# Gate folded into the output and query projections of a cross-attention block with a mixture of experts

## The reference

```python
# _layernorm(x): (x - mean) / sqrt(var + 1e-5)
x = x + xattn(ctx, ctx, _layernorm(x), mask, wq, bq, wk, bk, wv, bv, wo, bo)   # 16 heads of 16, ... @ wo_w + wo_b
x = x + ffn(_layernorm(x), rms_w, gate_w, W1, b1, W2, b2)

# inside ffn
xn = x * rsqrt(mean(x * x) + 1e-6) * rms_w
logits = xn @ gate_w.T                       # 8 experts
scores = softmax(logits)
top1_idx, top1_score = argmax(scores), max(scores)
ye = silu(xn @ W1[e] + b1[e]) @ W2[e] + b2[e]     # e = top1_idx, F = 1024
out = ye * top1_score
```

## Time and profile before

| | |
|---|---|
| median of 3 runs | 920.2 us (919.24 to 921.61) |
| the profiled execution | 914.09 us, its span 912.3 us |
| PE busy | 802.1 us, 88% |
| DVE busy | 620.0 us, 68% |
| POOL busy | 444.6 us, 49% |
| ACT busy | 430.2 us, 47% |
| chain that ended last, by engine | PE 33%, SP's queue 16%, POOL 16%, DMA 15%, issue 10%, DVE 7% |

### The profile page before, as it was taken

How to read it: one execution, slowest core, us unless ns; L and a number is a source line. 1 busy time by engine, 2 the same in 40 slices (tenths; PEclk the granted TensorE clock), 3 DMA queues, 4 the chain that set the end, 5 groups by cost and what they waited for, 6 DMA issues and landing times.

```text
span 912.3 us, 28391 instructions
## 1 busy us (share of the span) xinstructions
PE 802.1 (88%) x8764; PEld 586.7 (64%) x8764; DVE 620.0 (68%) x1898; ACT 430.2 (47%) x1004; POOL 444.6 (49%) x566
## 2 busy tenths in 40 slices
PE   1678999999999999999999999998627999999994
PEld 0445666666666666666666666665415888888783
DVE  4567777777777777777777877776374666665542
ACT  0235555555555555555555565554403333333331
POOL 0255644565445564456544665465416555556311
PEclk9989999999999999999999999999857999999998
DMA  4465676656776567765777567764153222223200
GB/s 134 108 169 134 171 175 182 177 142 169 180 186 175 142 164 181 204 195 153 196 191 215 165 168 193 195 189 120 32 195 95 77 82 82 81 79 97 71 29 7
DMA packets 107139, 130.01 MB, mean 143 GB/s; under 512 B 12942, under 2 KB 93704, under 8 KB 106569
## 3 DMA queue, kind: packets, MB, share of 16 engines
q1 hardware_dynamic: 100936, 116.38, 47.4%
q0 software_dynamic: 5600, 12.87, 4.7%
q10 hardware_dynamic: 544, 0.00, 0.0%
HBM read 94.07 MB, written 36.06 MB: 143 GB/s over the span
## 4 chain that ended last, share of the span: by engine, by line
PE 33%; SPq 16%; POOL 16%; DMA 15%; issue 10%; DVE 7%; ACT 1%; POOLq 1%; DVEq 0%
DMA arena_w<-in_x 14%; PE ps L1218 12%; PE ps L1236 10%; POOL arena_w L595 6%; SPq L476 5%; SPq L471 5%; POOL arena_b L583 3%; POOL arena_w L602 2%; POOL arena_w L584 2%; POOL arena_b L559 2%; SPq L440 1%; DVE arena_b L1351 1%; PE ps L1018 1%; POOL arena_b L584 1%; PE ps L994 1%
## 5 line engine op out<-in xcount | busy, mean ns | idle before, releaser
L744 ACT ACTIVATE arena_b<-ps 128x448 f32<-128x448 f32 (+1 forms) x384 | 194.0, 540 | 120.0 <-PE ps L980 119.1
L1369 DVE CUSTOM_DVE_ANT_0 arena_w<-ps,arena_w 112x375 bf16<-112x375 f32 x256 | 140.5, 549 | 47.4 <-PE ps L954 41.3
L976 PE MATMUL ps<-arena_b,arena_w 128*128 128x448 bf16 x384 | 136.6, 356 | 7.7 <-DVE arena_b L1378 5.6
L557 POOL TENSOR_TENSOR arena_b<-arena_b,arena_w 112x1 f32<-112x1 f32 x32 | 6.1, 190 | 279.8 <-DVE arena_b L1353 279.8
L1369 DVE CUSTOM_DVE_ANT_0 arena_b<-ps,arena_w 112x375 bf16<-112x375 f32 x256 | 139.8, 546 | 0.1
L980 PE MATMUL ps<-arena_b 128*128 128x224 f16 x768 | 136.2, 259 | 0.0
L1218 PE MATMUL ps<-arena_b,w_parts 128*128 128x256 f16 (+1 forms) x1056 | 109.2, 254 | 0.5 <-issue 0.3
L1218 PEld LDWEIGHTS ps<-arena_b,w_parts 128*128 x1056 | 90.8, 98 | 17.4 <-issue 2.9
L980 PEld LDWEIGHTS ps<-arena_b 128*128 128x128 f16 x768 | 75.2, 98 | 39.4
L994 PE MATMUL ps<-arena_b 128*17 128x112 f32 (+1 forms) x3072 | 99.4, 261 | 0.1
L1236 PE MATMUL ps<-arena_w,arena_b 128*128 x840 | 95.2, 273 | 0.1
(11 more groups left out here) (187 smaller groups left out, 1344.1 us busy)
## 6 DMA issues: line engine op xcount, KB each, us to landing
arena_b<-k_spill SPq DMA_DIRECT2D x128, 192.0 KB, 3.8
arena_b<-in_L_ffn_W SPq DMA_DIRECT2D x64, 256.0 KB, 4.5
arena_b<-q_spill SPq DMA_DIRECT2D x128, 112.0 KB, 4.2
k_spill<-arena_b SPq DMA_DIRECT2D x32, 384.0 KB, 5.0
arena_b<-in_ctx SPq DMA_DIRECT2D x32, 256.0 KB
arena_w<-in_x SPq DMA_DIRECT2D x64, 112.0 KB, 4.6
q_spill<-arena_w SPq DMA_DIRECT2D x32, 224.0 KB, 2.1
rows<-arena_w SPq DMA_DIRECT2D x32, 224.0 KB, 2.3
```

Of the source, the lines that this page charges most:

```text
L744: nc.scalar.activation(probsT[u % PROB_BUFFERS][0:n], scoreT_bank[c][0:n, 0:QUAD * T], ACT.Exp, scale=1.0 / SCALE_SCORES).then_inc(probs_r ...
L976: pe.matmul(bank[:, 0:QUAD * T], mask_keys[:, quad, c, :], max_rows[par].rearrange("p h t -> p (h t)"), start=True, stop=False)
L1369: nc.vector.tensor_tensor_reduce(out=masked_scores[r % 2], in0=shared_bank[r][0:T, 0:S], in1=mask_bias, scale=-1.0, scalar=3.4e38, op0=ALU ...
```

## The change

The logits are linear in x1, so they need not be computed from the normalised rows. With G the gate times rms_w, and G' the same with the mean over the 256 rows taken off each column, x1 @ G' equals (x1 - mean(x1)) @ G. The second scale is one factor per token, which changes no order among the 8 logits; it is needed only in the softmax value. x1 is x + attention @ wo + bo + (values' bias part). So:

- In setup G' is computed (a matmul with a constant 1/256, a subtraction), then wo @ G', which is appended to wo as 8 more columns, and a bias row; this needs wo transposed and one more load of bo.
- `project_attention` yields 264 columns; the last 8 are the attention's part of the logits.
- `project_queries` multiplies the transposed normalised x by G' too (8 columns). Normalised x is (x - mean) / std, so the result is multiplied by std, which POOL makes as variance times 1/std. DVE's `gate_of_x` does this and adds the bias row; `add_residual` adds the attention's part.
- The transposes, the gate's matmuls and two ACT copies per batch are gone; ACT keeps the factor of each batch (`copy_factor`), and POOL multiplies all logits by it once, before the exponential.

```diff
-        wo_sb = carve("a", P, DT, D)
+        wo_sb = carve("a", P, DT, WO_COLS)
# SP, setup
+            sp.dma_start(bo_cols, bo.rearrange("(t p) -> p t", p=P),
+                         allow_slow_non_contiguous=True).then_inc(weights_loaded, 16)
# POOL
-            def queries_rstd(b):
+            def queries_rstd(b, par):
...
                 pool.tensor_tensor(rstd, var1, minus_half, ALU.pow).then_inc(rstd_ready, 1)
+
+                wait_count(pool, gate_x_ready, b - 1)
+                pool.wait_ge(rstd_ready, b + 1)
+                pool.tensor_tensor(std1[par], var1, rstd, ALU.mult).then_inc(std_ready, 1)
...
+            pool.wait_ge(ln2_copied, B)
+            pool.wait_ge(logits_centred, 1)
+            pool.tensor_tensor(gate_exp, gate_exp, ln2_all[:, :].unsqueeze(2).to_broadcast([T, B, EXPERTS]),
+                               ALU.mult).then_inc(logits_centred, 1)
# ACT, setup and steps
+            nc.scalar.activation(woT.rearrange("p t n -> p (t n)"), scoreT_bank[0][:, 0:DT * D], ACT.Copy
+                                 ).then_inc(woT_copied, 1)
...
+            nc.scalar.activation(gate_bias, scoreT_bank[1][0:T, 0:EXPERTS], ACT.Copy).then_inc(setup_copied, 1)
...
-            def copy_routed(st):
...
-            def copy_gate(st):
...
+            def copy_factor(st):
                 b = st.batch(3)
+                wait_apart(act, ln2_rstd, b + 1, act_passed)
+                nc.scalar.activation(ln2_all[:, bass.ds(b, 1)], ln2, ACT.Copy).then_inc(ln2_copied, 1)
# PE, setup
+            for t in range(DT):
+                mm = pe.matmul(scoreT_bank[1][:, 0:EXPERTS], average, gw_sb[:, t], start=t == 0, stop=t == DT - 1)
+            mm.then_inc(gate_mean_ready, 1)
...
+            pe.wait_ge(wo_gate_copied, 1)
+            for j in range(DT):
+                pe.matmul(scoreT_bank[1][0:T, 0:EXPERTS], bv_rep[:, j, :], wo_sb[:, j, D:], start=j == 0, stop=False)
+            for j in range(DT):
+                mm = pe.matmul(scoreT_bank[1][0:T, 0:EXPERTS], bo_rep[:, j, :], gate_centre[:, j], start=False,
+                               stop=j == DT - 1)
+            mm.then_inc(gate_bias_ready, 1)
             pe.wait_ge(setup_copied, N_SETUP_COPIED)
# PE, scores of quad 3
                         pe.wait_ge(q_low_ready, DT * (b + 2))
+                        pe.wait_ge(gate_x_ready, b + 2)
                     if st.exists(2):
                         pe.wait_ge(x1_ready, st.batch(2) + 1)
-                    if st.exists(3):
-                        pe.wait_ge(xrT_copied, st.batch(3) + 1)
+                        pe.wait_ge(gate_added, st.batch(2) + 1)
# PE, project_queries
+                for k in range(DT):
+                    mm = pe.matmul(proj_bank[0][0:T, DT * T:DT * T + EXPERTS], xnT[:, k, :], gate_centre[:, k],
+                                   start=k == 0, stop=k == DT - 1)
                 mm.then_inc(queries_ready, 1)
# PE, project_attention
-                    mm = pe.matmul(tail_bank[0:T, 0:D], attT[:, j, :], wo_sb[:, j, :],
+                    mm = pe.matmul(tail_bank[0:T, 0:WO_COLS], attT[:, j, :], wo_sb[:, j, :],
...
-            def transpose_routed(st):
...
-            def gate(st):
# DVE, setup
+            nc.vector.tensor_copy(bo_rep, bo_cols.unsqueeze(2).to_broadcast([P, DT, T])).then_inc(const_dve, 1)
...
+            dve.wait_ge(gate_mean_ready, 1)
+            nc.vector.tensor_tensor(gate_centre, gw_sb, scoreT_bank[1][:, 0:EXPERTS].unsqueeze(1).to_broadcast(
+                [P, DT, EXPERTS]), ALU.subtract).then_inc(gate_centred, 1)
# DVE, steps
+            def gate_of_x(st):
+
+                b, par = st.batch(-1), st.parity(-1)
+                dve.wait_ge(std_ready, b + 1)
+                wait_apart(dve, queries_ready, b + 1, dve_passed)
+                nc.vector.scalar_tensor_tensor(
+                    out=gate_logits[:, bass.ds(b, 1), :].rearrange("p o e -> p (o e)"),
+                    in0=proj_bank[0][0:T, DT * T:DT * T + EXPERTS], scalar=std1[par], in1=gate_bias,
+                    op0=ALU.mult, op1=ALU.add).then_inc(gate_x_ready, 1)
...
                 nc.vector.tensor_tensor(row_tile[par][:, D:], tail_bank[0:T, 0:D], x_res[par], ALU.add).then_inc(x1_ready, 1)
+                logits = gate_logits[:, bass.ds(b, 1), :].rearrange("p o e -> p (o e)")
+                wait_apart(dve, gate_x_ready, b + 1, dve_passed)
+                nc.vector.tensor_tensor(logits, tail_bank[0:T, D:WO_COLS], logits, ALU.add).then_inc(gate_added, 1)
```

More of the change, by code:

```diff
@@ L55 @@
 ARENA_B = 18960
+WO_COLS = D + EXPERTS
 W_CHUNK = EXPERTS * DT * F // B
@@ L201, in build @@
         bv_rep = carve("a", P, DT, T)
+        gate_centre = carve("a", P, DT, EXPERTS)
+        gate_bias = carve("a", T, EXPERTS)
+        std1 = [carve("a", T, 1) for _ in range(2)]
+        bo_cols = carve("a", P, DT)
         bvo = carve("a", T, D)
@@ L385, in build @@
         centred_ready = sem("centred_ready")
-        xrT_ready = sem("xrT_ready")
-        xrT_copied = sem("xrT_copied")
-        gate_ready = sem("gate_ready")
-        gate_copied = sem("gate_copied")
+        ln2_copied = sem("ln2_copied")
+        std_ready = sem("std_ready")
+        gate_x_ready = sem("gate_x_ready")
+        gate_added = sem("gate_added")
+        woT_ready = sem("woT_ready")
+        woT_copied = sem("woT_copied")
+        gate_mean_ready = sem("gate_mean_ready")
+        gate_centred = sem("gate_centred")
+        wo_gate_ready = sem("wo_gate_ready")
+        wo_gate_copied = sem("wo_gate_copied")
+        gate_bias_ready = sem("gate_bias_ready")
         w_staged = [sem("w_staged0"), sem("w_staged1")]
@@ L427, in build @@
         block = stack.enter_context(nc.Block())
[L429 removed]
+        N_WEIGHTS = 13
         Q_MOVED, K_MOVED = 16 * len(GROUPS), 16 * len(GROUPS)
         N_CONST_POOL = 2
[L432 to L433 removed]
+        N_CONST_DVE = 29
+        N_SETUP_COPIED = 7
         CTX_LOADED = 16 * 2
@@ L669, in step @@
                 if st.exists(-2):
-                    queries_rstd(st.batch(-2))
+                    queries_rstd(st.batch(-2), st.parity(-2))
                 if st.exists(0):
@@ L834, in step @@
                     copy_values(st.batch(0), st.parity(0), 0)
+                if st.exists(3):
+                    copy_factor(st)
                 if st.exists(1):
@@ L903, in _ @@
             mm.then_inc(setup_pe, 1)
+            for j in range(DT):
+                for t in range(DT):
+                    mm = pe.transpose(scoreT_bank[0][:, j * D + t * P:j * D + (t + 1) * P], wo_sb[:, t, j * P:(j + 1) * P],
+                                      ident[:, :])
+            mm.then_inc(woT_ready, 1)
+            pe.wait_ge(const_dve, 8)
+            pe.wait_ge(setup_copied, DT)
+            for t in range(DT):
+                mm = pe.matmul(scoreT_bank[1][:, 0:EXPERTS], average, gw_sb[:, t], start=t == 0, stop=t == DT - 1)
+            mm.then_inc(gate_mean_ready, 1)
+            pe.wait_ge(woT_copied, 1)
+            pe.wait_ge(gate_centred, 1)
+            for t in range(DT):
+                for j in range(DT):
+                    mm = pe.matmul(scoreT_bank[2][:, t * EXPERTS:(t + 1) * EXPERTS], woT[:, j, t * P:(t + 1) * P],
+                                   gate_centre[:, j], start=j == 0, stop=j == DT - 1)
+            mm.then_inc(wo_gate_ready, 1)
             pe.wait_ge(const_dve, N_CONST_DVE)
             for j in range(DT):
-                mm = pe.matmul(proj_bank[0][0:T, 0:D], bv_rep[:, j, :], wo_sb[:, j, :], start=j == 0, stop=j == DT - 1)
+                mm = pe.matmul(proj_bank[0][0:T, 0:D], bv_rep[:, j, :], wo_sb[:, j, 0:D], start=j == 0, stop=j == DT - 1)
             mm.then_inc(setup_pe, 1)
             pe.matmul(proj_bank[1][:, 0:T], keep_ones, keep_diagonal, start=True, stop=True).then_inc(setup_pe, 1)
+            pe.wait_ge(wo_gate_copied, 1)
+            for j in range(DT):
+                pe.matmul(scoreT_bank[1][0:T, 0:EXPERTS], bv_rep[:, j, :], wo_sb[:, j, D:], start=j == 0, stop=False)
+            for j in range(DT):
+                mm = pe.matmul(scoreT_bank[1][0:T, 0:EXPERTS], bo_rep[:, j, :], gate_centre[:, j], start=False,
+                               stop=j == DT - 1)
+            mm.then_inc(gate_bias_ready, 1)
             pe.wait_ge(setup_copied, N_SETUP_COPIED)
@@ L927, in scores @@
                         pe.wait_ge(ctx_low_ready, DT * (b + 2))
-                    if st.exists(4):
-                        wait_count(pe, gate_copied, st.batch(3))
                 elif quad == 1:
@@ L1076, in project_attention @@
                 for j in range(DT):
-                    mm = pe.matmul(tail_bank[0:T, 0:D], attT[:, j, :], wo_sb[:, j, :],
+                    mm = pe.matmul(tail_bank[0:T, 0:WO_COLS], attT[:, j, :], wo_sb[:, j, :],
                                    start=j == 0, stop=j == DT - 1)
                 mm.then_inc(wo_ready, 1)
-            def transpose_routed(st):
-                b = st.batch(3)
-                bank_free(st, 2, 3)
```

(16 more changed lines are left out.)

47 lines of the change are left out of this document (22 added, 25 removed).

## The result

| | before | after |
|---|---|---|
| median of the runs, us | 920.31 (919.24 to 921.61, 6 runs) | 930.25 (925.94 to 932.96, 6 runs) |
| profiled execution / its span, us | 914.1 / 912.3 | 930.12 / 928.3 |

The ratio is 1.0104, with an interval of 1.008 to 1.0128; the forecast was 929.4. The profiled execution of before lay 6 us under the median of its runs, and the prediction had no term for that. The table sets the stages side by side. All are start times of instructions: the first context transpose, the mean and variance of x (`bn_stats`) of batches 4, 29 and 31, the first routing instruction.

The account below looks back on a forecast made before the run. The prediction took the loop through x's landing to bound the laps. Setup +2.1, first projections +1.2, laps +8.5, steps 28 and 29 +0.8, end -1.25 and -2.1 gave +9.2 on 920.2: 929.4 us, range 924 to 934 (8 in 10: 918 to 936).

Parts of the forecast that it names:

- What bounds the kernel: Attention laps: the x loop, x landing through DVE, POOL and SP's issues to the next landing, sets them, 19.04 us.
- POOL's product, +0.27 a lap: New variance times 1/std ahead of the split of W2, on the x path, uncovered: +0.27 us a lap (0.19 to 0.55).
- Laps, +8.5 in all: Attention stage: 15 laps up to 345.89 us at +0.27, 11 behind at +0.4; together +8.5 us (0 to 17).
- The second loop: DVE's maxima, freed banks, PE's context transposes, ACT, DVE: DVE's two additions +0.4, PE 0, from 18.7 to 19.1 us.
- L1385: DVE instruction held by POOL's split: later split lets it end some 0.65 us earlier, but L1344 starts as before.
- Rival 3: Laps: L1385 held a whole POOL instruction later, 0.67 us a lap in 26 laps, 17 us, total 938; chance 0.10.
- Rival 1: Laps: PE and freed banks set them, DVE's waits hide its additions, each step gains; total about 914; chance 0.13.
- Rival 2: Laps: x's time from issue to landing shrinks and eats POOL's 0.27 us; laps 0, total 920; chance 0.14.
- Setup, +2.1: Before the first context transpose: extra DMA issue 0.51, two DVE instructions 0.4, gate bias on PE 1.2; +2.1 us.
- first projections, +1.2: First queries' projection: four more PE passes +1.0 and the first DVE addition +0.2; +1.2 us (0.5 to 1.5).
- Steps 28 and 29: Two steps with no x to wait for: +0.4 us each, 0.8 together.
- The end, -3.35: From step 30, removed PE passes give -1.25 us; behind the last step, routing's wait for gate logits gone, -2.1.

Follow-up runs that it names:

- f1: Kernel before with POOL's masking of the queries moved ahead of the split of W2 and the residual; ratio to before 0.993, lap 18.62 us.
- h4: Kernel before, unchanged, run and traced a second time; 921.31 us (one run), lap 19.02 us.
- e2: Kernel before with only POOL's product variance times 1/std added behind 1/std, result unused; ratio to before 1.0109, lap 19.26 us.
- e4: Kernel before with its buffers placed as in the changed kernel, same instructions; ratio to before 1.0073, lap 19.10 us.
- g1: Changed kernel with 8 unused bytes ahead of the later small tiles, restoring the old places within 64 bytes; ratio to before 1.0131, lap 19.24 us.
- h1: f1 with two DVE instructions of 112x8 added and PE's waits on them, results unused; 938.98 us (one run), lap 18.67 us.
- h2: f1 with two eight-column matmuls (four PE passes) added ahead of the queries' signal, results unused; 952.25 us (one run), lap 18.99 us.
- f2: Changed kernel with POOL's masking of the queries moved ahead of the split of W2 and the residual; ratio to before 0.9981, lap 18.87 us.
- e3: Kernel before with only two DVE instructions of 112x8 added and PE's waits on them, results unused; ratio to before 1.003, lap 18.99 us.
- h3: Changed kernel, unaltered, run again; 969.5 us, ratio to before 1.0146, lap 19.47 us.

## Why the prediction held, and where it didn't

- **What bounds the kernel**: right. The x loop sets the laps, and f1 shows it by taking it away: 0.4 a lap below h4.
- **POOL's product, +0.27 a lap**: right, 0.26 alone (e2) and 0.32 in after.
- **Laps, +8.5 in all**: the mechanism was right for the x loop and the size too small, 12.0 against h4 (and over 25 laps; I had counted 26). Landings of x were to come 19.3 and 19.1 us apart and came 19.6 and 19.3 apart. Missing were 0.13 for the masking's place (e4, g1) and, by the trace alone, 0.05 in the split of W2 (L606 to L609 2.27 and 2.16 us, 2.22 and 2.11 before).
- **The second loop, "+0.4 from DVE, 0 for PE in the laps"**: this step failed, twice. DVE's instructions cost 0.05 there (h1), and PE's passes 0.37 (h2). I took DVE to be what the loop waits for in its densest stretch, and let the new passes act only through the high queries, under the cover of DVE's shortened L1385. In the traces of f1, h2 and f2 PE never pauses from the projection to the context's transposes, so its passes count by themselves, and DVE's additions go into DVE's wait for the scores. In after, too, the first maximum of the last quad was not 0.4 later against x, but 0.03. The size of the passes was too large as well: 0.48 in the row of the gate, and 0.37 a lap where they stand now (0.31 on h2's chain and some more in what follows). My 19.1 us for this loop should have been 18.87 (f2). Since x sets all laps, the term had no say: the later laps grew by the x loop's terms, as the earlier ones. That the 0.4 a lap I gave them for it came near the 0.48 that they grew by is luck.
- **L1385**: right in the main. 1.09 became 0.41, without the hold by the split's first instruction that I had left in, and most of the gain was eaten by the wait for ACT (0.44): L1379 started 0.16 earlier, where I had "as before". Perfetto Trace Analysis of the Trainium skill (Optimizing Scalar/DVE Operations) says that the two engines share a read port which a two-port DVE operation takes exclusively. In the rows of before it is DVE's instruction that waits out POOL's. In e2 L1385's counterpart, 0.16 ahead of the split's second instruction, took 1.35 us in the first half of the laps and 0.41 in the second, where POOL's took 1.15 in place of 1.04; what decides between the two is open.
- **Rival 3**, the longer hold, did not happen in the laps: from 130 us on after shows L1430 never above 0.42 (in the first steps up to 1.23). Where it did happen, in the first half of e2's laps, those grew by no more than POOL's product, 19.35 against h4's 19.13. **Rival 1**, with DVE hiding its additions, was true of them (e3, h1), but x still set the laps. **Rival 2**, a shorter landing: not seen, 4.90 and 4.60 us before and behind 346 us against h4's 4.83 and 4.67.
- **Setup, +2.1, and first projections, +1.2**: too high, +1.0 to +1.2 for the setup, and +1.0 to +1.9 for both by the issue of the first query spill (36.47 before and 36.67 in h4, 38.36 after and 37.62 in h3). I had doubled the eight-column pass to 0.24; it took 0.14 and 0.19 there, and 0.15 in the first projection of after.
- **Steps 28 and 29**: +0.6 in place of +0.8.
- **The end, -3.35**: -2.4 of it is the wait at routing, forecast -2.1; the late steps gave the rest, -1.2 against before and -2.2 against h4, forecast -1.25. The exponential ended at 677.27, 0.9 ahead of DVE's need at 678.16: covered, as forecast.

## What to carry to other kernels

Ask of every instruction that a change adds which loop it stands in and what was waiting there, and not how much work it takes away: this change removes PE work and lengthens every lap, because 0.3 us on POOL stood between a landing and the next load's issue. The PE work that it removed stood where another path was as long, and the four short passes that it added stand where PE never waits, so without the x loop it would have cost 0.25 a lap still. When a path through one engine sets the laps, look first at the order on that engine: moving the masking ahead of the split gave 0.7% where the change cost 1%. And a new small tile moves all tiles behind it, so compare the durations of untouched instructions too.

## What the runs showed of the hardware

- A POOL product of 128x448 halves took 976 ns with its tiles at bytes 56 and 8 of a block of 64, and 1042 ns at 48 and 0, between 155 and 560 us, in eight kernels and in four: 967 to 984 and 1034 to 1054 ns, without overlap.
- Four matmul passes of eight columns with 112 columns of fp32 weights take 0.47 us from first start to last end at a granted clock of 1.00 (h2), but put between other matmuls they delay these by 0.35 to 0.37 us, some 0.09 a pass.
- In the first steps (47 to 71 us) the granted clock was 0.86 and 1.00 in two executions of before, and 0.64 and 0.62 in two of after. Yet the stretch up to x of batch 4 took 60.18, 63.33, 64.27 and 64.49 us, out of step with it: the granted clock alone does not set this stage.
- The untouched stage of the experts took 218 us in some runs and 248 to 262 in others. From routing to the end the granted clock was 0.91 in the former and 0.87 to 0.90 in the others, too small a difference for 14 to 20% more time by itself. The cause is open; comparisons are safe only against the kernel before in the same runs, and best by stage.
